# A feed-forward stage with its rounding step in PSUM, one gate bank, and the residual summed in PSUM

## The reference

```python
def fp4_quant_dequant(x):                      # blocks of 16
    scale = max(|x| over the block) / 6
    q = nearest value of 0, .5, 1, 1.5, 2, 3, 4, 6 to x / scale
    return q * scale
x + fp4_linear(silu(fp4_linear(n, w_gate)) * fp4_linear(n, w_up), w_down)   # n = layernorm(x)
```

## Time and profile before

| what | value |
|---|---|
| median of 3 runs | 1041.48 us (1040.91 to 1042.05) |
| the profiled execution | 1041.14 us |
| its span, first to last instruction | 1039.4 us |
| VectorE busy over the span | 902.7 us (87%) |
| TensorE (PE) matmul busy | 950.2 us (91%) |
| ffn1 in the span | about 728 to 801 us |
| ffn2 in the span | about 975 to 1039 us |

### The profile page before, as it was taken

One profiled execution on the slowest core, in us unless ns is written; L12 is line 12 of the kernel. 1 busy time (PEld: TensorE's weight loads), 2 busy tenths in 40 slices (PEclk: granted clock), 3 DMA queues, 4 the chain that ended last, 5 costly groups with the idle time before them and its releaser, 6 DMA issues. The chain is left out here.

```text
span 1039.4 us, 29750 instructions
## 1 busy us (share of the span) xinstructions
PE 950.2 (91%) x11909; PEld 577.4 (56%) x11909; DVE 902.7 (87%) x1724; ACT 761.0 (73%) x1683; POOL 760.1 (73%) x426
## 2 busy tenths in 40 slices
PE   5799999999999999999999999987477899999775
PEld 2455555555555555555555565655256566666445
DVE  6889998999989999899998999998799657787597
ACT  5888898898988989889898898885333245555442
POOL 1688999989999999899998999997353323333243
PEclk9799999999999999999999999999798889999899
DMA  6845443544444444545445454430760110000001
GB/s 191 279 128 166 153 156 125 166 145 182 147 149 152 148 151 145 183 145 160 143 133 169 140 166 143 141 129 2 161 141 1 21 22 12 13 2 2 2 0 41
DMA packets 69272, 120.88 MB, mean 116 GB/s; under 512 B 40072, under 2 KB 51152, under 8 KB 60112
## 3 DMA queue, kind: packets, MB, share of 16 engines
q1 hardware_dynamic: 69136, 118.98, 36.3%
HBM read 111.10 MB, written 6.29 MB: 113 GB/s over the span
## 5 line engine op out<-in xcount | busy, mean ns | idle before, releaser
L902 DVE TENSOR_TENSOR_SCAN hid<-decay,acc 128x256 f32<-128x256 f32 x1024 | 604.6, 664 | 40.9 <-PE acc L539 40.5
L1002 POOL TENSOR_TENSOR prod<-hid,c_rep 128x1024 f32<-128x1024 f32 x256 | 600.1, 2373 | 44.3 <-DVE hid L902 33.3
L765 ACT ACTIVATE decay<-delta,a_neg 128x255 f32<-128x255 f32 x1024 | 428.2, 501 | 47.7 <-DVE hid L902 47.5
L539 PE MATMUL acc<-b_diag,du_t 64*64 64x256 f32 x4096 | 273.2, 383 | 15.9 <-DVE hid L902 12.2
L567 PE MATMUL ring<-prod,ident 64*64 64x256 f32 x4096 | 255.5, 379 | 2.2 <-POOL prod L1002 2.2
L539 PEld LDWEIGHTS acc<-b_diag,du_t 64*64 64x64 f32 x4096 | 147.8, 134 | 124.8 <-DVE hid L902 55.4
L567 PEld LDWEIGHTS ring<-prod,ident 64*64 64x64 f32 x4096 | 152.0, 133 | 83.5 <-issue 22.9
L1915 POOL TENSOR_SCALAR_AFFINE_SELECT att_probs<-att_probs 128x512 f32<-128x512 f32 x64 | 40.9, 639 | 109.3 <-ACT att_probs L1958 106.9
L1958 ACT ACTIVATE att_probs<-acc 128x384 f32<-128x384 f32 x128 | 55.8, 488 | 55.8 <-PE acc L1732 55.8
L444 PE MATMUL ring<-xpad,diag_cw 64*64 64x512 f32 x512 | 60.6, 590 | 0.0
L1116 POOL TENSOR_TENSOR ffn_h_value<-ffn_h,ffn_h_inv 128x704 f32<-128x704 f32 x16 | 23.7, 1479 | 43.5 <-DVE ffn_h_value L1139 32.5
(11 more groups left out here) (180 smaller groups left out, 1259.5 us busy)
## 6 DMA issues: line engine op xcount, KB each, us to landing
c_rep<-c_rows SPq DMA_DIRECT2D x64, 1024.0 KB, 4.8
b_diag<-diag_rows SPq DMA_DIRECT2D x62, 512.0 KB, 3.8
diag_rows<-zeros SPq DMA_DIRECT2D x2, 2048.0 KB, 12.4
att_qk<-in_pos_q SPq DMA_DIRECT2D x4, 768.0 KB
att_qk<-in_pos_k SPq DMA_DIRECT2D x4, 768.0 KB
att_qk<-att_dense SPq DMA_DIRECT2D x24, 64.0 KB
resid<-in_x SPq DMA_DIRECT2D x4, 256.0 KB, 3.2
c_rows<-bc SPq DMA_DIRECT2D x64, 8.0 KB, 1.5
```

Source lines behind the costliest of these rows:

```text
L539: last = nc.tensor.matmul(inj[m * HALF:(m + 1) * HALF, K % 2, at:at + HALF * SG], du_t[rows, n % 2, e, chans:chans + HALF], b_diag[rows, K ...
L765: last = nc.scalar.activation(decay[:, K % DECAYS, s, 1:], delta[:, n % 2, h, e * SEQ + 1:(e + 1) * SEQ], ACT.Exp, scale=a_neg[:, lay(n) % ...
L902: last = nc.vector.tensor_tensor_scan(hid[:, K % HIDS, s, :], decay[:, K % DECAYS, s, :], rows[:, s, :], 0.0, ALU.mult, ALU.add)
L1002: nc.gpsimd.tensor_tensor(prod[:, K // 2 % PRODS, h], hid[:, K % HIDS, :, :], c_rep[:, g, :, at], ALU.mult).then_inc(s_prod, 1)
```

## The change

The step of h is held in PSUM (`acc` banks 2 and 3, 704 columns); ScalarE writes it there once the value before has been rounded. There is one gate bank, one down bank, and the banks of turned h share `ring` 0 with turned x. The residual enters down as a product of the identity with `resid`, and ScalarE copies the sum back; VectorE's add is gone. The orders are rewritten: VectorE does exponent(k-1), hidden(k), round(k-1); TensorE gate_up(k+1), turn_h(k-2), down(k-3); ScalarE step(k-1), gate(k+1), copy_h(k-2), copy_down(k-3); GpSimd, once exponent(k-1) is done, dequant(k-2), normal(k). All four strips run in ffn1. In ffn2 the offset of the last chunk is computed after hidden(0), and ScalarE normalises that chunk after gate(0) and copy_x(1).

```diff
 def scalar_step(self, a, c):
+        if self.held is not None and c:
+            self.s_round.wait(a, "rounded", c - 1)
-        ...activation(self.step[:, i, :], self.step[:, i, :], ACT.Relu, ...
+        ...activation(self.steps(i), self.step[:, i, :], ACT.Relu, ...
-        gate_bank = [bank(ring, 1), bank(ring, 2)]
-        up_bank = [bank(ring, 3), bank(acc, 0)]
-        hT_bank = [bank(acc, 1)[:, 0:2 * P], bank(acc, 1)[:, 2 * P:4 * P], bank(acc, 2)[:, 0:2 * P]]
-        down_bank = [bank(acc, 3)[:, 0:2 * P], bank(ring, 0)[:, 0:2 * P]]
+        qh = Rounder(core, sb, "h", HCOLS // BLK, 4, acc[:, 2 * BANK:2 * BANK + HCOLS])
+        x_bank, gate_bank, up_bank = bank(ring, 0), bank(ring, 1), [bank(ring, 2), bank(acc, 0)]
+        hT_bank = [bank(ring, 0)[:, 0:2 * P], bank(ring, 0)[:, 2 * P:4 * P], bank(acc, 1)[:, 0:2 * P]]
+        down_bank = bank(ring, 3)[:, 0:2 * P]
 @block.vector
                 if early:
                     norm.vector_moments(v, 3)
-                    norm.vector_offset(v, 3)
-                    x.vector_scales(v, 3)
-                for k in range(HSTEPS + 3):
+                for k in range(HSTEPS + 1):
+                    if 1 <= k:
+                        qh.vector_exponent(v, k - 1)
+                    if k in (1, 3) and k // 2 + 2 >= early:
+                        x.q.vector_exponent(v, k // 2 + 2)
+                    if attention and k == HSTEPS - 1:
+                        v.wait_ge(s_add, 2)
+                        attention.norm.vector_moments(v, 0)
                     if k < HSTEPS:
                         hidden(k)
+                    if k == 0 and early:
+                        norm.vector_offset(v, 3)
+                    if k == 1:
                         x.vector_scales(v, 3)
+                    if attention and k == HSTEPS:
+                        attention.norm.vector_normalise(v, 0)
+                    if 1 <= k:
+                        qh.vector_round(v, k - 1)
 ...
 @block.gpsimd
+                for k in range(HSTEPS + 2):
+                    if k >= 2:
+                        p.wait_ge(qh.s_exponent, min(k, HSTEPS))
+                        h_dequant(k - 2)
+                    if k < HSTEPS:
+                        h_normal(k)
 ...
 @block.tensor
 def gate_up(k):
-                        need(t, s_silu, n - 1)
+                        need(t, s_silu, n)
 def turn_h(k):
+                    t.wait_ge(s_xTc, 3 if k < 2 else 4)
 def down(k):
-                    need(t, s_add, k - 1)
+                    need(t, s_add, k)
                     for i in range(2):
+                        at = down_bank[:, i * P:(i + 1) * P]
+                        nc.tensor.matmul(at, ident[:, :], core.resid[:, 2 * k + i, :], start=True, stop=False)
                         for j in range(FTILES):
 ...
-                for k in range(HSTEPS + 3):
+                for k in range(HSTEPS + 2):
                     if k + 1 < HSTEPS:
                         gate_up(k + 1)
                     if k in (2, 4):
                         turn_x(k // 2 + 1)
+                    if attention and k == HSTEPS:
+                        t.wait_ge(s_h, 2 * HSTEPS)
+                        attention.tensor_turn(t)
+                    if k >= 2:
+                        turn_h(k - 2)
                     if k >= 3:
-                        turn_h(k - 3)
-                    if k >= 4:
-                        down(k - 4)
+                        down(k - 3)
                 down(HSTEPS - 1)
 ...
 @block.scalar
+                def copy_down(k):
+                    a.wait_ge(s_down, k + 1)
+                    nc.scalar.activation(resid_flat[:, k * 2 * P:(k + 1) * 2 * P], down_bank, ACT.Copy).then_inc(s_add, 1)
                 if early:
                     copy_x(0)
                     norm.scalar_rstd(a, 3)
-                    norm.scalar_normalise(a, 3)
                     nc.scalar.preload_act_table_set(SILU)
 ...
                 gate(0)
                 copy_x(1)
+                if early:
+                    norm.scalar_normalise(a, 3)
 ...
+                    if k >= 2:
+                        copy_h(k - 2)
                     if k >= 3:
-                        copy_h(k - 3)
+                        copy_down(k - 3)
```

More of the change, by code:

```diff
@@ L1125, in vector_exponent, with steps @@
                                           ALU.bitwise_and).then_inc(self.s_exponent, 1)
+    def steps(self, i):
+        return self.step[:, i, :] if self.held is None else self.held
     def scalar_step(self, a, c):
@@ L1134, in vector_round @@
         nc, i = self.core.nc, c % self.depth
-        value, step = self.value[:, i, :], self.step[:, i, :]
+        value, step = self.value[:, i, :], self.steps(i)
         v.wait_ge(self.s_step, c + 1)
@@ L1316, in _ @@
                     attention.norm.vector_moments(v, 1)
-                for k in range(HSTEPS - 2, HSTEPS):
-                    add(k)
-                if attention:
+                    attention.wait(v)
+                    attention.vector_strips(v, 0)
                     attention.norm.vector_normalise(v, 1)
-                    attention.wait(v)
-                    for g in range(2):
+                    for g in range(1, HGROUPS):
                         attention.vector_strips(v, g)
@@ L1341, in _ @@
                     x.pool_normal(p, 2)
[L1342 to L1351, removed]
+                for k in range(HSTEPS + 2):
[4 more added lines that the diff above has]
+                        h_normal(k)
+                    if k == 1:
                         x.pool_normal(p, 3)
+                    if k in (1, 3) and k // 2 + 2 >= early:
+                        x.pool_dequant(p, k // 2 + 2)
             @block.tensor
@@ L1358, in turn_x @@
                     need(t, s_xTc, c)
+                    need(t, s_hTc, 2 if c == 3 else 0)
                     for i in range(CH_TILES):
-                        last = nc.tensor.transpose(ring[:, i * P:(i + 1) * P], x.xq[:, c, i * P:(i + 1) * P], ident[:, :])
+                        last = nc.tensor.transpose(x_bank[:, i * P:(i + 1) * P], x.xq[:, c, i * P:(i + 1) * P], ident[:, :])
                     last.then_inc(s_xT, 1)
@@ L1411, in _ @@
                     attention.wait(t)
-                    t.wait_ge(s_silu, 2 * HSTEPS)
-                    t.wait_ge(s_xTc, CHUNKS)
+                    t.wait_ge(s_hTc, HSTEPS)
+                    qh.s_round.wait(t, "rounded", HSTEPS - 1)
                     attention.tensor_strips(t, 0)
                     t.wait_ge(s_add, HSTEPS)
-                    attention.tensor_strips(t, 1)
+                    for g in range(1, HGROUPS):
+                        attention.tensor_strips(t, g)
             @block.scalar
@@ L1429, in gate @@
                         need(a, s_h, n - 1)
-                        nc.scalar.activation(silu[:, i, :], gate_bank[i][:, 0:FFN], ACT.Silu).then_inc(s_silu, 1)
+                        nc.scalar.activation(silu[:, i, :], gate_bank[:, 0:FFN], ACT.Silu).then_inc(s_silu, 1)
                 def copy_h(k):
@@ L1451, in _ @@
                 copy_x(1)
-                for k in range(HSTEPS + 3):
+                if early:
+                    norm.scalar_normalise(a, 3)
+                for k in range(HSTEPS + 2):
                     if 1 <= k <= HSTEPS:
                         qh.scalar_step(a, k - 1)
-                    if k in (0, 2) and k // 2 + 2 >= early:
+                    if k in (1, 3) and k // 2 + 2 >= early:
                         x.q.scalar_step(a, k // 2 + 2)
@@ L1799, in project_out @@
                     banks.fill(last, "proj", b)
-                for g in range(2, HGROUPS):
-                    tiles.tensor_strips(t, g)
                 project_v(0)
@@ L1869, in add_out @@
                     banks.read(nc.vector.tensor_tensor(at, at, banks.bank("proj", b)[:, 0:SEQ], ALU.add), "proj", b)
-                for g in range(2, HGROUPS):
-                    tiles.vector_strips(v, g)
                 values(0)
```

57 lines of the change are left out of this document (16 added, 41 removed).

## The result

The changed kernel takes 1058.05 us in the median of 4 runs (1049.97 to 1064.04), the kernel before 1041.2 (1040.76 to 1042.05): a ratio of 1.0167, 95% interval 1.0121 to 1.0212. That is 16.9 us slower, where 4.3 was forecast, and outside the range given. The runs of the changed kernel also lie 14 us apart, those of before 1.3 (in the 78 later runs of before, 1035.2 to 1048.4).

A forecast was written before the change was run, and what follows sets the result against it. It took VectorE to bound both feed-forward stages now, TensorE and silu their middle after the change. First stage +3.1 and second +1.2 made +4.3 us on 1041.14, so 1045.4 us; range 1037.5 to 1048.5.

The forecast's parts named there:

- the four products there: First stage, gate_up(3) after 4.2 us idle waiting for hidden(2): its four products were charged at 1.2 GHz.
- the walk through the second stage: Second stage: down(0) starts at 1004.6 as now, last down at 1035.8, stage +1.2 us.
- the waits for silu: Single gate bank: TensorE waits for silu between two tiles, 0.78 us lost per step with nothing to cover it.
- My bound: TensorE's clock: an idle time of 4.0 us lowers it, one of 2.37 us does not.
- The round of TensorE: Middle of each stage: TensorE's round is 5.61 us, more than VectorE's 4.85, so TensorE and silu become the bound.
- The spacings of down: Second stage: starts of down 7.0, 5.6, 5.6, 2.6, 5.0, 2.9 and 2.5 us apart, last down 30.4 us behind the first.
- The exit: First stage, first strip to first score: 10.6 us where it is 9.8 now, +0.8.
- Rounding from PSUM: VectorE's rounding reads the step from PSUM and does not wait for GpSimd; bounds 0 and 1.4 us per step.
- The second stage's late offset: Second stage: last chunk's offset ready at 983.8, scalar_normalise(3) holds gate(1) back, silu of tile 2 starts at 985.4.
- gate wait not exposed: Rival: the 0.78 us between tiles is not bare, TensorE's round is 4.83, time 1038 us; chance 0.2.
- The clock stays at its upper level: Rival: first stage +1.7, sum +2.9 us, or +2.1 (1043.2) if the exit's 0.8 is hidden too; chance 0.2.
- The third rival: The clock falls in the second stage's tail too, before turn_h(6): +1.7 us more, 1047.1 us; chance 0.15.

The follow-up runs named there:

- e13: The changed kernel with only 2 idle products (results nobody reads) ahead of the turn of the third attention chunk: 1051.89 us, ratio 1.0112.
- e6: The changed kernel with offset and normalise of the second stage's chunk 3 back in their old place, no idle products: 1059.68 us, ratio 1.0214.
- e2: The changed kernel with two gate banks again, and so the rounding step of h back in SBUF: 1062.76 us, ratio 1.0247.
- e3: The changed kernel with the rounding step of h back in SBUF and still one gate bank: 1068.28 us, ratio 1.028.
- e9: The kernel before with idle products in TensorE's waits in both feed-forward stages, 12 ahead of the first stage and 2 in attention: 1036.71 us, ratio 0.9968.
- e10: The changed kernel with idle products in TensorE's waits in both stages, 12 ahead of the first stage and 2 early in attention: 1037.37 us, ratio 0.9979.
- e16: e10 without the identity product, so the residual is left out of the result: 1043.63 us, ratio 1.0039.
- e15: e10 with the rounding step of h in SBUF again: 1054.56 us, ratio 1.0146.
- e5: The kernel before with one gate bank alone and idle products in the waits for silu: 1059.0 us, ratio 1.0204.

## Why the prediction was wrong

**The clock in the entries (the step that failed).** In the first stage I charged the lower clock "to the four products there", and in the walk through the second stage to none: down(0) was to start at 1004.6, 28.8 us behind the first gate product. It took 36.0 us, at a granted clock of 0.50 to 0.62 in stretches of 10 us; the low clock came in from attention and gave way for less than 4 us, around 996, where before was at full clock 4 us behind its first gate product. In the first entry the low clock lasted from 757.9 to some 767 and covered transposes and the next pair of gate and up product too. What was missing is that the waits for silu, 0.78 us per step in my own round, do not only cost their length: while they stand between the two tiles of every step and TensorE has little else to do, the clock that has fallen stays down. With them filled the entries are 28.4 and 29.75 us, so the clock costs 4.5 and 6.3 us there (3.2 by the unfilled second entry of e13), and 2.5 in the loop, of which the forecast had 1.7. The Trainium skill (TensorE: Matmul & The Clock Gate, "A second HAM failure mode: psum-queue depth-cycling") tells of short idle times between groups of matmuls that let the gate go up and down. The rows agree in part: the clock was up around 996 only, and then down from 998 to 1021 without a break.

My bound was drawn from two idle times, 4.00 us that lowered the clock and 2.37 that did not the earlier trace rows. In the trace after, the clock falls within the up product of 997.11, with nothing longer ahead of it than the pause of 2.00 us that ends at 996.41; and in before it falls at 826, with no pause over 1.12 us in the 10 us ahead. Both are shorter than the 2.37 that did no harm. The length of one pause does not decide it.

**Attention, which the forecast left at 164.2 us.** It cost 2.7 us in the profile. Its start, with score products of 17 rows, runs at the lower clock for 14 us even in the kernel before (0.77 over 820 to 850). That stands in the trace of before, and the prediction says nothing of it, as the change does not touch it. With the clock up at its start attention takes 160 us in both kernels. From one kernel to the next it takes 160 to 176 us in the profiles (160.1 in e6, 174.3 in e2, 176.0 in e3), with the same work. That the runs of one kernel differ by it too is likely, but not shown: each kernel has one profile.

**What held.** The round of TensorE: 5.63 against 5.61. The spacings of down in the second stage, forecast 7.0, 5.6, 5.6, 2.6, 5.0, 2.9, 2.5: from the timeline 7.04, 5.63, 5.63, 2.59, 5.04, 2.82, 2.59. The exit, 10.75 against 10.6. Rounding from PSUM does not wait for GpSimd: all 32 rounding operations on h take 0.88 or 0.89 us, where in before 4 of the 16 of L1137 took up to 2.08. The second stage's late offset: silu of tile 2 starts 10.6 us behind the first gate product (forecast 9.6, at full clock). TensorE is the bound of the middle: VectorE now waits for the step, 12.4 us in 9 waits, as the trace has it for L1143:

```profile
  ACT acc L1136: 12.4, 9
```

The rival "gate wait not exposed" fell: the wait is bare in every round. "The clock stays at its upper level" fell as well, but e9 and e10 are its test: with the clock held up in both the change costs 0.7 us, where the sum had 2.9. The parts are not as forecast, though: against e9, e10's first entry is 3.7 us shorter and its loop 2.2 longer, where the forecast had 1.7 and 3.9. The third rival had the right mechanism, the clock, in the wrong place: the tail of the second stage ran at full clock (2.38 us idle, then transposes of 0.44).

**In one sum**, from the profiles of after and e10: 4.5 + 2.5 + 7.1 + 6.3 = 20.4 us of the 21.3 between them go with the clock, in first entry, loop, attention and second entry. Between before and e9 it is 4.0 us in attention and nothing elsewhere. The difference, about 16 us, is the slowdown that was measured.

**What stays open.** Which activity exactly raises or lowers the clock is not settled: e16 and e10 have the same idle products, and one fell at 810 to 820 and the other did not; e6 and before have the same wait in attention, and only in before the clock fell. So why attention took 2.7 us more than in before is open. That the runs of one kernel differ by their clock is shown by each run's mean clock; in which stage each of them lost it is known only for the profiled ones. Filling the unused waits ahead of 820 as well was not tried.

## What to carry to other kernels

A short wait put into every step can cost twice: its length, and the clock of what runs between the waits, in stretches where TensorE does little else. So price a change that thins out TensorE's work at both clock levels, and read the granted clock by stretch, in untouched stages too, before calling any of them unchanged. When a kernel's runs spread by more than a per cent, fill TensorE's waits with products that nobody reads and compare again: two such products took 0.3% off the kernel before, and with all of them in place a slowdown of 17 us shrank to less than one. Then check by the granted clock that it was held: in e13, e15 and e16 it was not, and their times alone would have misled.

## What the runs showed of the hardware

Idle products of some 0.6 us in waits of 0.55 to 8.6 us took the mean granted clock from 0.950 to 0.984 and the time from 1058 to 1037 us. The wait of 1.1 us in attention was followed by a fall of the clock in before and by none in e6. TensorE counts as busy for 28.28 of 30 us both where it gets 0.77 of the clock (before) and where it gets all of it (e6), so the busy share does not show the loss; the weight loads done do (293 and 353). An operation of VectorE with both inputs in SBUF took 1957 ns beside GpSimd's multiply and 886 with one in PSUM, same shape. With one gate bank and filled pauses the first entry took 45.0 us in one order of the queues (e5) and 28.4 in another (e10).
